# Two attentions and two FFNs, pipelined over batches: projections of attention A in two alternating PSUM banks, its contexts summed by DVE, v as a plain fp32 product, three norms on POOL

## The reference, cut to what matters

```
x = x + attn_a(layernorm(x))     # 16 heads of 64: q softmax over channels, k softmax over tokens,
                                 # context = q^T k per head, out = context v, then w_out and a bias
x = x + ffn(layernorm(x))        # r = sigmoid(W_r mix), k = relu(W_k mix)^2, out = r * (W_v k);
                                 # mix = mu * x_t + (1 - mu) * x_(t-1)
x = x + attn_b(layernorm(x))     # 16 heads of 8, rotary q and k, softmax over 512 keys, W_O
x = x + ffn(layernorm(x))
```

## Time and profile before

| | |
|---|---|
| Median of 3 runs | 992.31 us (991.56 to 995.57) |
| Profiled execution, its own time | 995.63 us |
| Its span, first to last instruction | 993.8 us |
| Mean granted TensorE clock | 0.981 |
| Busy, share of span | PE 92%, ACT 68%, DVE 65%, PEld 54%, POOL 51% |
| DMA moved | 87.64 MB, 88 GB/s in the mean |

### The profile page before, as it was taken

The page is one execution under the profiler, slowest core; times in us unless marked ns, Lnnn a source line. Parts: engine busy times, 40 slices in busy tenths (PEclk is TensorE's granted clock), DMA queues, the critical chain, the costliest instruction groups (busy, mean ns, idle before and its releaser), DMA issues.

```text
span 993.8 us, 24338 instructions
## 1 busy us (share of the span) xinstructions
PE 915.5 (92%) x9807; PEld 532.9 (54%) x9807; DVE 645.1 (65%) x1546; ACT 673.9 (68%) x670; POOL 505.0 (51%) x345
## 2 busy tenths in 40 slices
PE   4987998999999999999999999999999999889983
PEld 3766554556565655555555555555555565433332
DVE  4777565668577766868677767858667566653234
ACT  4565667776767777777777777777676777567860
POOL 3758384645646564546647554555646454424100
PEclk9999799999999999999999999999999999899995
DMA  5012143324142423324142323423232323223310
GB/s 166 23 33 94 59 127 88 104 75 128 57 131 64 128 63 103 112 65 128 54 138 66 101 93 91 123 58 126 64 118 68 102 89 99 84 64 107 86 32 16
DMA packets 68685, 87.64 MB, mean 88 GB/s; under 512 B 13649, under 2 KB 40146, under 8 KB 68562
## 3 DMA queue, kind: packets, MB, share of 16 engines
q1 hardware_dynamic: 68562, 85.96, 28.6%
HBM read 16.19 MB, written 20.97 MB: 37 GB/s over the span
## 4 chain that ended last, share of the span: by engine, by line
PE 64%; DVE 13%; ACT 13%; issue 5%; SPq 2%; POOL 1%; DMA 1%; ACTq 0%; DVEq 0%
PE PS L1657 17%; PE PS L1613 9%; PE PS L1449 8%; ACT work L716 7%; PE PS L1451 5%; PE PS L1450 5%; PE PS L1517 5%; PE PS L1563 4%; DVE cT L1132 3%; ACT work_b L716 3%; DVE cT L1134 3%; PE PS L1557 3%; PE PS L1444 2%; PE PS L1546 2%; PE PS L1630 2%
## 5 line engine op out<-in xcount | busy, mean ns | idle before, releaser
L716 ACT ACTIVATE work<-PS 128x2048 f32<-128x2048 f32 x150 | 281.5, 1877 | 53.3 <-PE PS L1613 53.3
L706 ACT ACTIVATE work<-PS 128x512 f32<-128x512 f32 x256 | 152.6, 599 | 175.8 <-PE PS L1451 173.9
L464 POOL TENSOR_TENSOR rs<-ve,half_neg 128x4 f32<-128x4 f32 x64 | 64.8, 1012 | 332.4 <-DVE ve L932 332.4
L1657 PE MATMUL PS<-work,v 128*32 128x512 f32 x1368 | 175.5, 606 | 0.5 <-ACT work L723 0.5
L477 POOL TENSOR_TENSOR work<-work,q_rcp 128x1024 f32<-128x1024 f32 x64 | 122.2, 1910 | 97.0 <-DVE q_rcp L984 59.0
L716 ACT ACTIVATE work_b<-PS 128x2048 f32<-128x2048 f32 x74 | 138.9, 1877 | 25.0 <-PE PS L1613 25.0
L1613 PE MATMUL PS<-q_st,k_st 32*128 32x512 f32 x896 | 114.7, 500 | 18.1 <-ACT work L716 8.2
L1449 PE MATMUL PS<-wqk,h1h 128*128 128x512 f32 x256 | 125.3, 489 | 5.7 <-issue 2.6
L1451 PE MATMUL PS<-wqk,h1l 128*128 128x512 f32 x256 | 101.8, 398 | 0.0
L1450 PE MATMUL PS<-wqk,h1h 128*128 128x512 f32 x256 | 101.7, 397 | 0.0
L1051 DVE SCALAR_TENSOR_TENSOR gated<-gate,PS 128x512 f32<-128x512 f32 x31 | 21.3, 687 | 109.1 <-PE PS L1570 109.1
(11 more groups left out here) (174 smaller groups left out, 1654.7 us busy)
## 6 DMA issues: line engine op xcount, KB each, us to landing
qkv_scratch<-qkv_sb SPq DMA_DIRECT2D x16, 768.0 KB, 4.5
rot<-qkv_sb SPq DMA_DIRECT2D x32, 256.0 KB, 2.4
k_st<-qk_hi SPq DMA_DIRECT2D x128, 64.0 KB, 2.1
q_st<-qk_hi SPq DMA_DIRECT2D x128, 64.0 KB, 2.2
k_st<-qk_lo SPq DMA_DIRECT2D x128, 64.0 KB, 2.1
q_st<-qk_lo SPq DMA_DIRECT2D x128, 64.0 KB, 2.1
parted<-U SPq DMA_DIRECT2D x52, 128.0 KB, 2.9
xa<-in_attn_a_x SPq DMA_DIRECT2D x16, 256.0 KB, 3.2
```

The lines of the kernel that those rows point to most:

```text
L464: pool.tensor_tensor(rs[:, :], ve[:, :], half_neg[:, :], ALU.pow).then_inc(rstd[n].sem, 1)
L706: act.activation((EQ, EK)[r // 2][c % 2][:, (r % 2) * 512:(r % 2) * 512 + 512], PS[:, bank, :], ACT.Exp)\
L716: act.activation(probs_of(z, b, n), PS[:, 0:4, :], ACT.Exp).then_inc(z["s_exp"].sem, 1)
L1657: mm = pe.matmul(PS[32 * h:32 * h + 32, 6, :], v_flat[p][:, kc, at:at + 32], probs_of(z, b, n)[:, h, :], start=(n % 8 == 0), stop=(n % 8 = ...
```

## The change

It alters the paired steps and what they need; the filling and draining steps keep their order. SP's list of DMAs is not touched.

- **Banks.** proj_half n goes into bank 4 or 5 by turns and waits for half n - 2 to be read instead of half n - 1. The one-off products move to bank 7 (some to 4 or 5 where no half is in them).
- **Contexts.** Each context product starts its own sum (`stop=True`) in bank 5, and six DVE operations (c_add) copy or add the parts into `ctx_sum` in SBUF. The halves after them wait for that (`c_sum`). The column sums and the scaling (c_totals, c_norm) then read `ctx_sum`. The first context moves from part 4 to part 3 of a step, the last from part 1 to part 0.
- **v of attention B** is four plain fp32 products of 128 x 128 from h3 and W7T instead of twelve f32r ones; DVE writes one more copy of the transposed h3 from bank 7.
- **Norms.** In paired steps the first, second and third norm are applied by POOL, as two TENSOR_TENSORs over 128 x 512 each, and no longer by four DVE TENSOR_SCALARs.
- **Orders.** On ACT both A exponentials of a part come after both score exponentials, and the copy of k moves to DVE, after c_norm. t_copy moves from part 2 to part 1. On DVE, divide comes between the copies of k and v. On POOL the rotary products come ahead of q_hats 0 and the first norm.

```diff
+            def ln_apply(n, j, src, dst, taken):                      # POOL
+                hold(pool, taken, j - 1)
+                pool.tensor_tensor(dst, src, mean broadcast, ALU.subtract)
+                hold(pool, rstd[n], j)
+                pool.tensor_tensor(dst, dst, rs broadcast, ALU.mult)
...
             def proj_half(a, p, n, alone):
-                hold(pe, ph_exp, a, n - 3 if alone else n)
-                bank = n % 4 if alone else 4
+                hold(pe, ph_exp, a, n - 3 if alone else max(n - 1, 0))
+                bank = n % 4 if alone else 4 + n % 2
...
             def proj_b(j, c, bank=7):
                 else:
-                        mm = halves(PS[:, bank, t * D:t * D + D], (h3h[:, tok], h3l[:, tok]), (w3h[:, cols], w3l[:, cols]))
+                        mm = pe.matmul(PS[:, bank, t * D:t * D + D], h3[:, t, :], W7T[:, 5, :], start=True, stop=True)
...
+            def c_add(i, n):                                          # DVE
+                pairs = (range(0, 8), range(0, 4), range(4, 8), range(0, 4), range(4, 8), range(0, 8))[n]
+                hold(dve, c_mm, i, (2, 3, 4, 5, 6, 8)[n])
+                if n == 0:
+                    dve.tensor_copy(at, part).then_inc(c_sum.sem, 1)
+                else:
+                    hold(dve, c_sum, i, n)
+                    dve.tensor_tensor(at, part, at, ALU.add).then_inc(c_sum.sem, 1)
...
             # DVE, paired step with all stages; lines with a sign changed or moved
                     split_h3(l)                      # now three copies
                     pv_copy(z, e, 1)
+                    c_add(s, 5); c_totals(s, ctx_sum)
                     qkv_free(l)
                     p_copy(l, 0)
+                    c_norm(s, ctx_sum)
+                    p_copy(l, 1, other)
+                    divide(z, e)
+                    p_copy(l, 2, 5 if A else 4)
+                    look_at(parted[:, 1, :], e, AX_X, 2)
+                m_copy(s, 7)
                 sums_of(a, 0)
+                ln1_stats(a + 1); add_x1(s, 7); add_x3(z, e, other)
                 sums_of(a, 1)
+                c_add(a, 0); h1_copy(a + 1, 1 - p); scale_and_mix(f1, s); c_add(a, 1)
                 pv_copy(z, b, 0); relu(f1, s, other)
+                x3_stats(z, 3, e)
                 sums_of(a, 2)
+                c_add(a, 2)
                 gate_v(f1, s, other)
...
             # POOL, paired step
                 add_bias(s)
                 rope_by_cos(z, l); rope_by_sin(z, l); rope_sum(z, l)
                 q_hats(a, 0)
+                rsqrt_var(0, a + 1); ln_apply(0, a + 1, xa, h1, h1_T)
+                rsqrt_var(1, s); ln_apply(1, s, x1, hn1, f1["hT"])
                 q_hats(a, 1)
                 split_h1(a + 1, 1 - p); split_qk(z, l); square(f1, s); v_copy(z, l, p)
                 rsqrt_var(3, e); ln3_apply(e)
                 q_hats(a, 2); rsqrt_var(2, s); square(f2, e)
+                ln_apply(2, s, x2, h3, p_mm)
                 q_hats(a, 3)
...
             # PE, paired step with all stages, what stands in each part beside scores and weighed values
+            k0: context(s, 3) | proj_b 0 -> 7, half 0, half 1, proj_b 1 -> 7
+            k1: ctx_wout | half 2, proj_b 2 (v) -> 5, wv_ctx_wout -> 7, hold p_ev(l, 3), half 3
+            k2: | attn_out -> 7, half 4, half 5, hold x1_ok, heads_out -> 7
+            k3: context 0 | hold x3_ok, head_T, half 6, hold c_sum 1, half 7, hold h1_sb, ffn_T(f1)
+            k4: context 1a | half 8, ffn_k -> 7, half 9, hold ph_exp 9, ffn_r -> 4
+            k5: context 1b | ffn_v -> 7, hold gate, half 10, half 11, ffn_T(f2) after the norm of x3
+            k6: context 2a | half 12, ffn_k(f2), half 13, hold ph_exp 13, ffn_r(f2) -> 4
+            k7: context 2b | ffn_v(f2), hold gate, half 14, half 15, h3_transposes
```

More of the change, by code:

```diff
@@ L618, in paired_step @@
                     rope_sum(z, l)
-                if there(a + 1):
+                if E and there(a + 1):
                     split_h1(a + 1, 1 - p)
+                split_qk(z, l)
+                hold(pool, f1["v"], s - 1)
+                square(f1, s)
+                if not E and there(a + 1):
+                    split_h1(a + 1, 1 - p)
+                hold(pool, p_ev, l)
+                hold(pool, z["pv"], l - 2)
+                v_copy(z, l, p)
                 if E:
                     rsqrt_var(3, e)
-                hold(pool, f1["v"], s - 1)
-                square(f1, s)
-                if E:
                     ln3_apply(e)
@@ L1256, in paired_step @@
                 if there(a + 1):
-                    ln1_norm(a + 1)
+                    ln1_stats(a + 1)
+                add_x1(s, 7 if A else 5)
                 if E:
-                    c_norm(s)
-                    p_copy(l, 2)
-                    divide(z, e)
-                    look_at(parted[:, 1, :], e, AX_X, 2)
-                else:
-                    qkv_free(l)
-                    p_copy(l, 0)
+                    add_x3(z, e, other)
+                else:
                     p_copy(l, 1)
-                m_copy(s)
-                add_x1(s)
                 if A:
                     sums_of(a, 1)
-                ln_norm(1, s, x1, hn1)
-                if there(a + 1):
+                    c_add(a, 0)
+                if E and there(a + 1):
                     h1_copy(a + 1, 1 - p)
-                if E:
-                    add_x3(z, e)
+                if not E:
+                    p_copy(l, 2)
                 scale_and_mix(f1, s)
-                if E:
-                    x3_stats(z, 3, e)
+                if A:
+                    c_add(a, 1)
                 pv_copy(z, b, 0)
@@ L1840, in paired_step @@
-                    if k == 1:
-                        hold(pe, p_ev, l, 1 if not E else 3 if A else 2)
-                        ctx_wout(s, (5, other), spacer=False)
-                    if k == 2:
-                        attn_out(s, 1 - p)
-                        if not E:
-                            proj_b(l, 2)
-                    if k == 3:
-                        if there(a + 1):
+                    if k == 7 and A:
+                        hold(pe, ph_exp, a, 14)
+                        context_narrow(a, 2, range(4, 8))
@@ new lines, in paired_step @@
+                    if k == 2:
+                        attn_out(s, 1 - p, 7 if A else 5)
+                        if A:
+                            proj_half(a, p, 4, False)
+                            proj_half(a, p, 5, False)
+                            hold(pe, x1_ok, s)
+                        else:
+                            hold(pe, p_ev, l)
+                        if E:
+                            heads_out(z, e, other)
+                        else:
+                            proj_b(l, 1)
@@ new lines, in paired_step @@
+                    if k == 6:
+                        if A:
+                            proj_half(a, p, 12, False)
+                        if E:
+                            if A:
+                                hold(pe, f2["mix"], e)
+                            else:
+                                hold(pe, f1["x"], s, 1)
+                            ffn_k(f2, e, other)
+                        if A:
+                            hold(pe, c_sum, a, 4)
+                            proj_half(a, p, 13, False)
+                        if E:
+                            if A:
+                                hold(pe, ph_exp, a, 13)
+                            ffn_r(f2, e, None, 4 if A else 7)
```

362 lines of the change are left out of this document (207 added, 155 removed).

## The result

The changed kernel takes 1037.4 us (median of 4 runs, 1030.4 to 1040.2) where the kernel before takes 992.7 on the same chip: a ratio of 1.0435, with a 95% interval of 1.038 to 1.049. It is slower by 4.35%; the prediction had 973, and a range of 950 to 1001. The profiled execution took 1037.2 us, its span is 1035.4.

A forecast was written before the change was run, and what follows sets the result against it. PE's list, twelve full steps of 56.39 us, was taken as the bound. Per step 56.4 - 3.7 + 1.2 + 0.7 + 0.4 = 55.0, 17 us over twelve; with iterations 3 and 16, 992.3 - 19 = 973 us, range 950 to 1001.

The forecast's parts named there:

- New wait 2, part 5: PE at ffn_T(f2) waits for the norm of x3 from POOL: 0.7 us a step, bounds nothing to 2.4.
- New wait 1, part 1: PE at half 3 (bank 5) waits for v's copy, behind divide on DVE, which needs `parted`: 1.2 us a step.
- the product of divide: DVE in part 1: gets in ahead of rope_sum on POOL, 0.6 us of run time and 0.2 of waiting.
- The third rival: Divide's product on DVE loses to POOL's rope_sum: 2.4 us more each step, 1002 us in all; chance 0.15.
- What PE gains in a full step: Bank waits 1.8, waits before scores 0.8, v 0.4, halves side by side 0.65: 3.7 us, a floor of 52.7.
- smaller waits: PE at heads_out, half 7, ffn_T(f1) and the two ffn_r in bank 4: together 0.4 us a step.
- the first rival: All new waits are covered, only 0.4 remains: 53.1 us per step, 950 us in all; chance 0.23.
- v's term: On PE, four plain fp32 products replace twelve short f32r passes, 0.88 for 1.29 us: gain 0.4.
- both ffn_r: On PE, the two ffn_r in bank 4 wait about 0.1 us each for the half before.
- What is added elsewhere: DVE some 42 us of 55, POOL 37.8, ACT loses 0.5; by load none overtakes PE.
- The granted clock: Full steps: the forecast is wrong if their granted clock falls below 1.00.
- Iteration 3: Outside the twelve full steps: gains about 1 us, from v and an earlier ctx_wout.

The follow-up runs named there:

- e11: Changed kernel with the last stack's DMAs reading from the resident weights, so split_qk's hold ends with stack 2, order kept: 993.1 us, 0.999.
- e1: Changed kernel with split_qk and v_copy back behind square, ln3_apply and q_hats 2 on POOL in paired steps: 982.9 us, 0.985.
- e10: Kernel before with only the change's earlier place of split_qk and v_copy in POOL's list: 1039.7 us, 1.050.
- e12: Changed kernel with square(f1) ahead of split_qk on POOL, v_copy, rstd 3 and ln3_apply still behind it: 1052.8 us, 1.059.
- e5: e1 with SP issuing part_values of e between the k stacks and the q stacks instead of behind all eight: 957.7 us, 0.962.
- e6: e5 with SP issuing stack 2 of k and q ahead of swap_pairs in iteration 3 alone: 951.4 us, 0.957.
- e8: e5 with the three norms given back to DVE: 967.3 us.
- e4: Changed kernel with only the three norms given back to DVE, as four TENSOR_SCALARs each: 1040.7 us, 1.050.

## Why the prediction was wrong

**The step that failed is "New wait 2, part 5".** It said that "POOL runs split_qk, square and v_copy back to back", followed both lists and had PE wait 0.7 us, 2.4 at most. POOL does not run them back to back: split_qk is the first of them, and it holds for the landing of the last stack, which SP issues last in its step. I had counted each instruction of split_qk at its new place and had not asked what it waits for there. In the kernel before the hold lay behind square, rstd 3, the norm and q_hats, by when the stack had long landed. Part 5 came to 3.35 us above the 6.08 that it takes without the wait, and part 6 to 0.67 more on average by the half-clock stretches; together 4.0 where the prediction had 0.7. e11 shows it most directly: with the hold on the last stack gone and the order kept, part 5 stands 0.65 us above 6.08, which is the 0.7 of the prediction, and the time is 993.1. e1 (order back) agrees. e10 shows that the move is dear in the kernel before too, in another way, and e12 that a late split_qk is as dear when the hold is covered.

**"New wait 1, part 1"** was right in its mechanism and too small. Predicted and measured, from the start of the step: `parted` landed at 10 and 9.96; RECIPROCAL ended at 13.4 and 13.3; half 3 could have started at 13.6 and 14.0; the product ended at 14 and 15.4; v's copy at 14.8 and 16.0. The error is in the product of divide alone, the term of 0.6 plus 0.2. swap_pairs landed at 12.5 instead of 11.2, so that rope_by_sin, which the prediction had over by 13.6, ran until 14.9 and held the product itself. Its issue was as predicted, 1.3 behind that of `parted` (ended 8.8 and 7.6 into the step); what was longer is the time from issue to landing, in the median of all 2.4 in before and 3.1 in after, of nine full steps 2.5 and 3.6. The row of the kernel before, and the row of the kernel after:

```profile
rot<-qkv_sb SPq DMA_DIRECT2D x32, 256.0 KB, 2.4
```

```profile
rot<-qkv_sb SPq DMA_DIRECT2D x32, 256.0 KB, 3.1
```

Over twelve steps part 1 lies 1.9 us above its 8.03, against 1.2 predicted. The third rival priced this race, against the wrong one of POOL's two instructions.

**What PE gains in a full step** was right as a sum. The parts without new waits sum, with part 1 at 8.03 and part 5 at 6.08, to 6.60 + 8.03 + 6.36 + 6.03 + 6.86 + 6.08 + 6.87 + 6.08 = 52.9, beside a predicted floor of 52.7 and 0.4 of smaller waits. e5 reaches 53.2 in a step and e6, with 951.4 us, the first rival's 950. v's term was 0.4 and measured 0.45; no run has the other terms singly. One of them was too large: both ffn_r still come 0.49 and 0.48 behind the pass before them, as in the kernel before (0.48), now waiting for ACT to read bank 4. That is 0.25 each where the prediction left 0.1, so something else gave a little more than its term, and that the sum is right to 0.2 is in part luck.

**What is added elsewhere** was right in kind. POOL has 38.4 us in a step of after, predicted 37.8. DVE has 47.0, predicted 42; 43.4 in e5, where it is blocked less. Neither became the bound by load, and e8 shows that moving the norms to POOL was a gain; e4 lies too near to after to tell.

**The granted clock** stood among the conditions of failure, as it should. It adds 1.6 us to part 6 in five steps and 0.83 to part 2 in three, 10.6 us of the 33.5 us (12 x 2.79) that the full steps grew.

**Iteration 3** was predicted to gain 1 and lost 7.2: 5.5 us are the queue of SP at swap_pairs (e5 to e6) and 3.7 the place of split_qk (after to e1, 65.6 to 62.0); against them stands a gain of 2.2 (58.4 in before, 56.2 in e6). New wait 1 has no part in it, since iteration 3 has no divide. I had not walked it, since it has no part_values.

The sum closes with e11, which is the changed kernel without the overlooked hold. Its full step is 56.2 where the forecast had 55.0: 0.8 more in part 1 (2.0 for 1.2), 0.6 in part 2 by the clock, nothing in part 5, and 0.2 less in the rest. That is 12 x 1.2 = 14 us, and iteration 3 adds 5.1 (62.5 us, forecast 58.4 - 1 = 57.4). So 973 becomes 992; e11 measured 993.1. Of the 64 us that the forecast missed, the hold is 44. The 55.4 of e1 lies nearer to the 55.0, but by offset: it has no wait in part 5 (forecast 0.7), 0.9 more in part 1 and 0.4 in part 2.

What stays open: whether the last stack's hold could be removed by a second pair of buffers wasn't tried. And why the clock falls behind some groups of waits in part 5 and not behind others of the same length was not settled.

## What to carry to other kernels

When an instruction is moved earlier on an in-order engine, list what it holds for at the new place, also the transfers that still read what it overwrites; its duration is the smaller part of its price. Ask also what runs beside it at the time to which the hold puts it: here it was DVE's statistics, with their consumers behind them. Where a walk ends with a margin of tenths of a microsecond on the landing of a DMA, price both outcomes and try a reordering of the issues first: two edits of the queue here were worth 31 us, while the reordering of DVE's list passed the wait on and cost 25 to 33. And walk the irregular iterations too: iteration 3 alone lost 7.2 us, as much as 2.6 full steps.

## What the hardware showed that was not expected

- Waits of PE of 1 to 2 us each can be paid twice. In e1, without them in part 5, part 6 is 6.87 in all twelve steps; in after it is 8.5 in five, each with a stretch at a granted clock of 0.50.
- Instructions of DVE on 128x4 elements, 0.15 us each when alone, took 0.95 to 2.28 us beside POOL's (four of seven in part 5's timeline); TENSOR_SCALARs too, though the prediction gave all seven two inputs in SBUF. A chain of seven such took 5.7 us (557.10 to 562.8), where e10 has the first five in 0.6.
- The same transfer of 256 KB took a different time from issue to landing by the order of what stands around it: `rot` 2.4 us in before, 2.8 in e5, 3.1 in after. What of the order makes it was not separated.
